# Gated cross-attention decoder, two layers: the second attention's keys and values made in their own stage, from a stored transposed context, with one joint product of query and key weights

## What is computed

```python
# x, ctx: (128, 64, 128) f32; every "+" below is onto the residual x
x = x + tanh(g_xattn[0]) * L0_xattn(layernorm(x), ctx, ctx, mask0, ...)   # 16 heads of 8 channels
x = x + tanh(g_ffn[0])   * L0_ffn(layernorm(x), ...)                      # 8 experts, the best 2 per token
x = x + tanh(g_xattn[1]) * L1_xattn(layernorm(x), ctx, ctx, mask1, Wq, bq, Wk, bk, Wv, bv)
x = x + tanh(g_ffn[1])   * L1_ffn(layernorm(x), W1, b1, W2, b2)           # quantised to 8 bits

def _L1_xattn_ref(q, k, v, mask, Wq, bq, Wk, bk, Wv, bv):
    Qp = q @ Wq + bq
    Kp = k @ Wk + bk
    Vp = jnp.tanh(v @ Wv + bv)
    qk = jnp.einsum('bqd,bkd->bqk', Qp, Kp)
    qk = qk + mask[:, None, :].astype(qk.dtype)
    attn = jax.nn.softmax(qk, axis=-1)
    return jnp.einsum('bqk,bkd->bqd', attn, Vp)
```

## Time and profile before

| | us |
|---|---|
| median of the timed executions | 821.13 |
| lowest and highest of three | 815.74 to 821.61 |
| span of the profiled execution, the only time that the page gives of it | 881.7 |
| PE busy in it | 708.1 |
| DVE busy | 710.4 |
| POOL busy | 585.0 |
| ACT busy | 566.2 |

### The profile page before, as it was taken

How to read it: one execution, slowest core, us unless ns; L and a number is a source line. 1 busy time by engine, 2 the same in 40 slices (tenths; PEclk the granted TensorE clock), 3 DMA queues, 4 the chain that set the end, 5 groups by cost and what they waited for, 6 DMA issues and landing times. The chain is left out here.

```text
span 881.7 us, 19709 instructions
## 1 busy us (share of the span) xinstructions
PE 708.1 (80%) x6550; PEld 550.0 (62%) x6550; DVE 710.4 (81%) x1855; ACT 566.2 (64%) x1172; POOL 585.0 (66%) x570
## 2 busy tenths in 40 slices
PE   6998999999998998699369978988984789476435
PEld 3776777777776776577247767877872567233134
DVE  4999988888888998489166757767876899889988
ACT  4666566767676664576046656666766787488756
POOL 4675588888887788677746544656555898188810
PEclk9999899999999999899769989999996999755759
DMA  8414532323232222757348778878775933000005
GB/s 241 137 38 141 109 129 66 134 68 131 96 104 80 91 97 103 256 169 227 115 144 266 225 205 252 253 249 256 232 235 174 353 98 108 15 1 0 1 24 169
DMA packets 95430, 127.69 MB, mean 145 GB/s; under 512 B 20529, under 2 KB 65153, under 8 KB 94305
## 3 DMA queue, kind: packets, MB, share of 16 engines
q1 hardware_dynamic: 85760, 108.00, 40.0%
q0 software_dynamic: 8672, 17.99, 5.9%
q10 hardware_dynamic: 896, 0.43, 0.2%
HBM read 82.76 MB, written 43.53 MB: 143 GB/s over the span
## 5 line engine op out<-in xcount | busy, mean ns | idle before, releaser
L590 POOL DMA_INDIRECT m_results<-a_probs,e_to x142 | 146.9, 1035 | 106.6 <-ACT a_probs L827 59.4
L614 POOL TENSOR_TENSOR a_probs<-a_probs,a_top 128x1024 f32<-128x1024 f32 x64 | 122.0, 1906 | 57.0 <-DVE a_top L1682 56.0
L805 ACT ACTIVATE room<-a_ps_s,e_bias 128x512 f32<-128x512 f32 (+1 forms) x160 | 102.0, 652 | 85.8 <-PE a_ps_s L1111 54.8
L571 POOL DMA_INDIRECT m_tokens_to<-r_rows,r_place x128 | 133.9, 1046 | 32.3 <-issue 32.1
L1702 DVE CAST e_hp<-room 128x512 fp32r<-128x512 f32 (+1 forms) x160 | 67.8, 424 | 78.7 <-remote 32.2
L722 ACT ACTIVATE a_probs_t<-a_ps_pt 128x512 f32<-128x512 f32 x128 | 69.8, 592 | 84.5 <-PE a_ps_pt L1011 84.1
L1704 DVE TENSOR_TENSOR e_hp<-room,e_hp 128x512 fp32r<-128x512 f32 (+1 forms) x160 | 102.8, 643 | 5.5
L1634 DVE TENSOR_TENSOR a_probs<-a_ps_s,a_mask 128x1024 f32<-128x1024 f32 x64 | 77.9, 1217 | 13.4 <-PE a_ps_s L892 7.5
L995 PEld LDWEIGHTS a_ps_o<-a_vals,a_probs_t 128*64 128x64 f32 x2048 | 69.3, 140 | 30.0 <-issue 29.0
L995 PE MATMUL a_ps_o<-a_vals,a_probs_t 128*64 128x18 f32 x2048 | 77.2, 214 | 8.2 <-issue 7.0
L1682 DVE TENSOR_REDUCE a_top<-a_probs 128x16 f32<-128x1024 f32 x64 | 77.2, 1206 | 0.1
(11 more groups left out here) (422 smaller groups left out, 1901.6 us busy)
## 6 DMA issues: line engine op xcount, KB each, us to landing
e_weights<-m_weights_to SPq DMA_DIRECT2D x80, 512.0 KB
m_weights_to<-r_parts SPq DMA_DIRECT2D x8, 1024.0 KB
room<-m_tokens_to SPq DMA_DIRECT2D x31, 264.0 KB
c_two<-m_results SPq DMA_DIRECT2D x3, 1536.0 KB, 10.8
a_ctx_in<-in_ctx_dram SPq DMA_DIRECT2D x17, 256.0 KB, 2.8
m_keys_t<-n_keys SPq DMA_DIRECT2D x16, 256.0 KB
m_values<-n_values SPq DMA_DIRECT2D x16, 256.0 KB
out_dram<-x_all SPq DMA_DIRECT2D x15, 256.0 KB, 2.4
```

Of the source, the lines that this page charges most:

```text
L571: pool.indirect_dma_start(tokens_to, bass.IndirectOffsetOnAxis(ap=place[:, k, q:q + 1], axis=0), rows[:, c % RING, q % CT, k, :], None).th ...
L590: pool.indirect_dma_start(results, bass.IndirectOffsetOnAxis(ap=to[:, v, r:r + 1], axis=0), y[:, v, r], None).then_inc(returned[v], 16)
L614: pool.tensor_tensor(probs[:, j], probs[:, j], top[:, j].unsqueeze(2).broadcast_to([P, HEADS, SEQ]), ALU.subtract).then_inc(shifted, 1)
L805: act.activation(h[:, c, at], ps_h[c][:, at], ACT.Gelu_apprx_tanh, bias=bias[:, n % ROWS, c:c + 1]).then_inc(h_sb, 1)
```

## The change

The first attention makes no keys and values for the second. What it stores instead is the transposed context itself, straight from `ctx_t`, 256 KB per super-tile, in one DRAM buffer `context_t` instead of two; the 17th context turn is gone. ACT's copy into `ctx_t`, which has still one buffer, now waits for the store of the super-tile before (`context_out`). The weights of the second attention are loaded during the experts (six loads at `EARLY + 6`) and not at the start.

At the end of the experts PE transposes the query and the key weights, DVE adds a shift to the transposed query weights, and PE makes one joint matrix of both, 128x128, and a joint bias column. The key of the second attention is then the joint matrix times the context, and the query is the normalised x plus 1 alone: x has mean 0 over its 128 channels, so that adding 1 to each channel and `(bq - sum of a column of Wq) / 128` to each entry of that column's weights gives the query bias. Queries as a product are gone; a product for keys of the same size stands in their place. The values are made per step from the same context: a bf16 product of 512 columns puts the bias, in three bf16 parts, into PSUM, four f32 products of 128 follow, and ACT applies the tanh on the way out. Transposed x, keys and values have two buffers each, the context four; SP loads 256 KB per step (before: 512).

The splits' first waits for the stores of keys and values become waits for rows sent earlier (`sent`).

```diff
@@ SP, first attention @@
 def load_ctx(n):
-    if n > SUPERS:
+    if n >= SUPERS:
         return
...
-def store_keys(v):
-    at = ST * ((v + 1) % SUPERS)
-    sp.wait_ge(k1_sb, v + 1)
-    sp.dma_start(g["keys_t"][:, at:at + ST], keys1[:, v % 2]).then_inc(keys_out[v % 2], 16)
+def store_context(n):
+    sp.wait_ge(ct_sb, n + 1)
+    sp.dma_start(g["context_t"][:, ST * n:ST * n + ST], ctx_t[:]).then_inc(context_out, 16)
...
 for s in range(0, SUPERS):
     load_ctx(s + CTX_RING)
+    store_context(s)
...
-    if s:
-        store_keys(s - 1)
-        store_values(s - 1)
@@ SP, experts @@
     if n == EARLY + 6:
...
+        for dst, name in ((g["wq1"][:], "Wq"), (wk1[:], "Wk"), (g["wv1"][:], "Wv")):
+            sp.dma_start(dst, d["L1_xattn_" + name]).then_inc(next_in, 16)
...
-for u in range(2):
-    sp.wait_ge(keys_out[u], 16 * SUPERS // 2)
-    sp.wait_ge(values_out[u], 16 * SUPERS // 2)
+sp.wait_ge(context_out, 16 * SUPERS)
...
+for n, name in enumerate(("keys0", "values0")):
+    sp.dma_start(g[name][:], g["context_t"][:, ST * n:ST * n + ST]).then_inc(ahead_in, 16)
@@ ACT, first attention @@
 def copy_context(n):
     act.wait_ge(ct_ps, n + 1)
+    if n:
+        act.wait_ge(context_out, 16 * n)
     act.activation(ctx_t[:], flat(ps_1), ACT.Copy).then_inc(ct_sb, 1)
...
-                if j == 2:
-                    if s == 0:
-                        act.wait_ge(kv_in, 64)
-                    next_keys(s)
...
-                if j == 3:
-                    tanh_values(s)
@@ PE, first attention @@
 def values(n):
     pe.wait_ge(k_sb, n * 4 + 4)
-    if n:
-        pe.wait_ge(k1_sb, n)
...
-                    if j == 2:
-                        pe.wait_ge(v1_raw, s + 1)
...
-                if j == 2:
-                    next_keys(s)
...
-                if j == 1:
-                    pe.wait_ge(pt_sb, exps_of(t - 2) - 1) if t >= 2 else pe.wait_ge(q_sb, 1)
-                    next_values(s)
@@ PE, end of the experts @@
+            if t == ETILES - 1:
+                pe.wait_ge(next_in, 96)
+                pe.transpose(ps_1[:, 0], g["wq1"][:], ident[:])
+                pe.transpose(ps_1[:, 1], wk1[:], ident[:]).then_inc(both_pe, 1)
...
+        pe.wait_ge(both_dve, 5)
+        pe.matmul(ps_1[:, 2], wk1[:], wq_t[:], start=True, stop=True)
+        pe.matmul(ps_1[:, 3, 0:1], wq_t[:], bk1[:], start=True, stop=True).then_inc(both_pe, 1)
@@ DVE @@
-                if j == 2:
-                    next_values(s)
...
+        def shifted_queries():
+            dve.wait_ge(both_pe, 1)
+            dve.tensor_reduce(shift[:], ps_1[:, 0], AX_X, ALU.add).then_inc(both_dve, 1)
+            dve.tensor_copy(wk1[:], ps_1[:, 1]).then_inc(both_dve, 1)
...
+            dve.tensor_scalar(wq_t[:], ps_1[:, 0], shift[:, 0:1], None, ALU.add).then_inc(both_dve, 1)
...
+        def weights_of_both():
+            dve.wait_ge(both_pe, 2)
+            dve.tensor_copy(g["wq1"][:], ps_1[:, 2]).then_inc(both_dve, 1)
+            dve.tensor_copy(g["bq1"][:], ps_1[:, 3, 0:1]).then_inc(both_dve, 1)
...
+        shifted_queries()
+        values_bias()
@@ ACT, second attention @@
+            act.activation(xn_t[:, n % 2], ps_x[:].rearrange("p a b -> p (a b)"), ACT.Identity, bias=eps[:, 1:2])\
+                .then_inc(xt_sb, 1)
...
+        def tanh_values(n):
+            act.wait_ge(v_ps, n + 1)
+            if n >= 2:
+                act.wait_ge(o_ps, n - 1)
+            act.activation(vals[:, n % 2], ps_v[:], ACT.Tanh).then_inc(v_sb, 1)
...
+            if s < SUPERS:
+                tanh_values(s)
             if s in (2, 5):
                 roots({2: 2, 5: 3}[s])
@@ PE, second attention @@
-            pe.matmul(ps_q[:].rearrange("p a b -> p (a b)"), wq[:], xn_t[:], start=True, stop=True).then_inc(q_ps, 1)
+        def keys_of(n):
+            if n >= 2:
+                pe.wait_ge(c_in[n % DEEP], nth_load(n))
+            if n:
+                pe.wait_ge(k_sb, n)
+            pe.matmul(ps_k[:].rearrange("p a b -> p (a b)"), w_both[:], context[n % DEEP][:], start=True, stop=True)\
+                .then_inc(k_ps, 1)
+
+        def values_of(n):
+            if n:
+                pe.wait_ge(v_sb, n)
+            pe.matmul(ps_v[:].rearrange("p a b -> p (a b)"), g["ones_row"][:], g["bv_rows"][:].rearrange("p k c -> p (k c)"),
+                      start=True, stop=False)
+            for k in range(QUAD):
+                mm = pe.matmul(ps_v[:, k], context[n % DEEP][:, P * k:P * k + P], g["wv1"][:], start=False, stop=(k == QUAD - 1))
+            mm.then_inc(v_ps, 1)
...
             if s + 1 < SUPERS:
-                queries(s + 1)
+                keys_of(s + 1)
+            if s < SUPERS:
+                values_of(s)
             if s >= 1:
                 pe.wait_ge(pt_sb, s)
-                if s >= 2:
-                    pe.wait_ge(v_in[(s - 1) % DEEP], nth_load(s - 1))
+                pe.wait_ge(v_sb, s)
```

198 lines of the change are left out of this document (79 added, 119 removed).

## The result

The changed kernel has a median of 833.65 us (827.96 to 836.55 over four runs) against 820.2 us for the kernel before (815.74 to 821.61, four runs as well): a ratio of 1.0176, with a 95% interval from 1.0136 to 1.0216. The forecast was 814.1 us, with a range from 802 to 829: the measured time lies outside it, and on the other side of no change.

A forecast was written before the change was run, and what follows sets the result against it. It took PE, DVE and POOL as close limits in the first attention and DVE as the second's; terms summed to -7.5 us on a span of 881.7, scaled to the 821.13 us median: 814.1 us, range 802 to 829.

The forecast's parts named there:

- Bounds per super-tile of 4 to 15: at least DVE's 0.68: First attention: each super-tile gains at least DVE's removed 0.68 us, at most the 1.9 us POOL lets through.
- I take 1.15, between both ends: First attention, super-tiles 4 to 15: gain of 1.15 us each, -13.8 us over twelve (8 to 23).
- rival (b): First attention: freed PE becomes idle because POOL, and nearly DVE, are full; second attention pays fully; 827.9 us, chance 0.23.
- Super-tile 0: First attention's start: ACT's second context copy waits for the first store, offset by removed work; 0 (-2 to +4).
- the 2.8 us that were set against it: Super-tile 0: removed PE work (2.26 us) and DVE work (0.68) taken to offset the new store wait of +2.8 us.
- Super-tiles 1 to 3: First attention, no rows sent on POOL: gain of 1.0 us each, nearer to DVE's bound; -3.0 us (2 to 6).
- the experts' begin: Start of the experts: two last stores and a 17th context turn go; -1.5 us (0 to -3).
- The experts: Experts: only six small weight loads added on SP's queue; +0.5 us (0 to +3).
- Between the stages: After the last split: 15 operations at 0.25 us, 3.7 us, partly hidden in DVE's waits; +2.4 us (0 to +4).
- Second attention: PE's step grows from 3.92 to 5.03 us and becomes the limit instead of DVE; +7.9 us (+3 to +14).
- The step of under 4.8: Second attention: PE steps under 4.8 us, instead of 5.03, would show the account of PE wrong.
- The clock: Second attention: a fuller PE would run at 1.00 instead of 0.97, making the term 6.9 instead of 7.9 us.

The follow-up runs named there:

- e7: Changed kernel with the eight DVE operations splitting the values' bias spread over expert tiles 26 to 33; 833.91 us.
- e8: Changed kernel with one idle keys-sized PE product per super-tile in the first attention, ahead of the third tile's transpose of heads; 829.61 us.
- e3: Changed kernel with five idle PE products per super-tile in the first attention, sized and placed like the removed keys and values; 831.92 us.
- e1: The kernel before, unedited, profiled a second time; 817.4 us, span 815.7.
- e2: Changed kernel with two buffers for the transposed context in the first attention; 832.3 us.
- e4: Changed kernel without the four products of context and value weights per step of the second attention; 827.81 us.
- c1: Changed kernel with two transposed-context buffers, one idle keys-sized product per super-tile, and the values' bias split during the experts; 821.46 us.
- h1: Kernel before with joint weights made at its start and used for the first attention's next keys, second attention's query product removed; 822.15 us, ratio 1.0033.
- e5: Changed kernel with PE's query product moved ahead of the transpose of heads in each super-tile's third tile; 832.17 us.

## Why the prediction was wrong, point by point

- **First attention, super-tiles 4 to 14.** The step that failed is "Bounds per super-tile of 4 to 15: at least DVE's 0.68", and with it "I take 1.15, between both ends". Eleven super-tiles were to gain 12.7 us; they lost 3.2 (0.4 in e7's profile, with the same code in this stage). The reckoning took durations as fixed and bounded the gain from below by a gain. But removed work can leave PE waiting, and behind such a wait its clock can fall, as at 163.48 us above. With the clock kept (e8, e3) the gain is 2.3 and 2.7 us over eleven, 0.2 per super-tile, under DVE's 0.68 as well. This is the prediction's rival (b), the freed PE becomes idle: chance 0.23, and right in kind, though not in its reason, a full POOL: POOL's waits for DVE's maximum rose from 13.0 to 16.3 us. Its 827.9 us had 0 for this stretch, where 3.2 were lost, and nothing for super-tile 0, where it was 5.6; its other misses nearly cancel.
- **Why so little even at full clock.** PE, DVE and POOL are full to 94, 91 and 84% (super-tiles 4 to 14 of e1) and hand a tile round in a chain: scores, maximum, subtraction, transposes, products, division, heads, output, next heads. That the engines' busy times lie near the length of the super-tile was read as several limits close together, of which one is relieved. The rows fit a chain in which PE's removed work turned into waits for DVE: PE's wait at the heads rose from 7.4 to 24.6 us when it went. Which engine of the chain sets the 20.8 us of a super-tile at full clock was not tried; e3 shows only that it is not PE. PE's waits for DVE, which were the sign of it, stand in e1's two rows above, 4.8 and 7.3 us.
- **Super-tile 0.** Said to be 0 (-2 to +4), it was +5.6. The mechanism was right, the landing of the store was put at 25 us and came at 27; and the 2.8 us that were set against it, since this super-tile loses work too, did not come: even without the wait, in e2, super-tile 1 begins only 0.7 us ahead of e1. The Trainium skill, DMA: Bandwidth & Descriptors, section "Queues, rings and completion order", on transfers being taken in the order in which they were put in the ring (when they are down is not ordered by it): the trace agrees as far as it goes. The store issued at 22.13 us was down at 26.94, behind the last of the x loads issued ahead of it (25.54) and ahead of the load issued next (27.04). That is 4.8 us from its issue, where the page of the profile gives 2.6 us as the median of all sixteen context stores.
- **Super-tiles 1 to 3** gained 0.8, not 3.0; **the experts' begin** lost 0.9 together with super-tile 15, not -1.5 and -1.15. **The experts** took 3.4 us less, where +0.5 was said; in the ten other profiled variants they lie between 229.1 and 232.9 us, so at least half of this is spread.
- **Between the stages.** +2.4 said, +3.3 measured: the operations cost 0.27 each, near the estimated 0.25. What was wrong is the share that is hidden. By e7 the five of the shift and the two copies cost nothing, and the eight of the bias, back to back ahead of the rows that set the end, more than their own time.
- **Second attention.** +7.9 said, +6.9 measured in the profile (up to +9.4 in e2). The mechanism was right, PE is late with a step of 4.85 us (5.03 said), and e4 shows it. The two long steps came nearly as said too (7.02 and 7.07 us, 7.2 said). The step of under 4.8 that would have refuted the account did not come.
- **The clock.** The prediction weighed the Trainium skill, TensorE: Matmul & The Clock Gate, section "What's actually happening" (activity releases the throttle), only for the second attention, where it expected 1.00 of a fuller PE. The trace agrees in part: 0.98 instead of 0.95 in the changed kernel, but 0.95 in e2, e7 and c1, with the same instructions. The same rule, turned round, warns of every removal of PE work at a wait; it was left out of the first attention's sum, where it made a small gain a loss. Nor does it make the forecast right by itself: with the clock kept, 2.3 to 2.7 us of the 12.7 come.
- **The base.** A trace 7% over the timed runs was scaled down by a share. The excess was not a share: of 66 us 54 lay in the experts, 5.8 in super-tiles 4 to 14, 5.5 between these and the experts, and 0.4 in the second attention.

## What to carry to other kernels

Ahead of counting removed work on an engine as gained, look what that engine waits for right behind it: if the next instruction waits for another engine, the work was filling that wait. On TensorE a wait that grows can cost twice, because the instructions behind it can run at half speed; one product that nobody reads, put in the wait, cost nothing here and shortened the stretch by 2.7 to 6.2 us, and four per step took back all of h1's loss. Work that is moved from a stage where it fills waits to one where TensorE is full is paid: 5.0 of the second attention's 6.9 us were the four value products.

## What the runs showed of the hardware that was not expected

- 31 us of additional TensorE work (e3) did not lengthen the kernel, and 15 us less of it (h1) lengthened one stretch by 6.1 us, with the granted clock at 0.83 instead of 0.95.
- Behind a wait of 1.84 us of TensorE the instructions took about twice their time for 6 to 7 us; behind one of 0.98 us at the same place in e8 they did not. But behind one of 1.87 us in the changed kernel they did not either, and in e5 the clock was 0.92 with only two waits over 1.3 us in eleven super-tiles. The length of the last wait alone does not decide it; what does stays open.
- A repair can vanish from the total while its stretch shows it in full: e2 and e7 won 6.3 and 3.4 us at their places, and 1.4 and nothing in the median. In their profiles the clock fell elsewhere, at the second table load of the second attention among other places (7.07 or about 8.4 us for the same step; 8.4 to 8.5 in e2, e3 and e7). Together with e8 they gave 12.2 us, more than the three medians added up (1.4, -0.3 and 4.0). Why the clock falls there in some variants and not in others stays open.
